# Flamingo gated block on one Trainium2 core: LayerNorm statistics of x blocks 1 to 3 taken in steps 0 and 1 of segment 0, and context block 1 copied out between the first two exponentials

## What is computed

```python
x = x + tanh(g_xattn[0]) * xattn(layernorm(x), ctx_1024, ...)
x = x + tanh(g_ffn[0]) * ffn(layernorm(x), w_gate, w_up, w_down)
# xattn: 16 heads of 64
lat = layernorm(latents, ln_l_w, ln_l_b)     # latents: layernorm(x)
ctx = layernorm(context, ln_c_w, ln_c_b)
q = lat @ Wq;  k, v = split(ctx @ Wkv)
attn = softmax(clip(q @ k.T * 64**-0.5, -11, 11))
out = (attn @ v) @ Wo + bo
# ffn: fake-quantised gate, up and down products, 768 wide
```

## Time and profile before

| | |
|---|---|
| Time, median of 3 runs | 1176.95 us (1175.2 to 1177.44) |
| Profiled execution, its own time | 1177.15 us |
| Its span | 1175.3 us, 20655 instructions |
| PE busy | 1098.6 us, 93% |
| DVE busy | 976.0 us, 83% |
| ACT busy | 622.0 us, 53% |
| POOL busy | 34.1 us, 3% |
| DMA | 22.24 MB, mean 19 GB/s |
| PE clock granted, mean | 0.979 of full |

### The profile page before, as it was taken

One profiled execution on the slowest core, in us unless ns is written; L12 is line 12 of the kernel. 1 busy time (PEld: TensorE's weight loads), 2 busy tenths in 40 slices (PEclk: granted clock), 3 DMA queues, 4 the chain that ended last, 5 costly groups with the idle time before them and its releaser, 6 DMA issues.

```text
span 1175.3 us, 20655 instructions
## 1 busy us (share of the span) xinstructions
PE 1098.6 (93%) x8548; PEld 507.3 (43%) x8548; DVE 976.0 (83%) x1336; ACT 622.0 (53%) x719; POOL 34.1 (3%) x41
## 2 busy tenths in 40 slices
PE   5899999999999999999999999999999998999049
PEld 3443344434443444344434443444333332787049
DVE  7667978797879788988989888987888899849996
ACT  3455555555555555555555555555555555449652
POOL 0400000000000000000000000000000000003200
PEclk9999999999999999999999999999999999999579
DMA  5000300010001000100010001000000000000002
GB/s 168 1 1 2 117 1 19 1 37 2 20 1 37 1 19 2 37 1 20 1 37 1 20 1 38 1 20 1 20 10 11 10 11 10 1 1 1 0 1 73
DMA packets 27324, 22.24 MB, mean 19 GB/s; under 512 B 8477, under 2 KB 23006, under 8 KB 27230
## 3 DMA queue, kind: packets, MB, share of 16 engines
q1 hardware_dynamic: 27230, 20.92, 5.8%
HBM read 18.55 MB, written 2.22 MB: 18 GB/s over the span
## 4 chain that ended last, share of the span: by engine, by line
PE 81%; DVE 7%; ACT 4%; issue 4%; POOL 0%; POOLq 0%; DVEq 0%; ACTq 0%
PE ps L1145 29%; PE ps L1129 28%; PE ps L1028 5%; PE ps L1081 4%; PE ps L1038 3%; PE ps L1047 3%; PE ps L1247 3%; PE ps L1292 3%; DVE acc L785 2%; PE ps L1058 1%; DVE gt L955 1%; ACT z L609 1%; ACT z L611 1%; DVE e_buf L829 1%; DVE fst L672 1%
## 5 line engine op out<-in xcount | busy, mean ns | idle before, releaser
L531 ACT ACTIVATE e_buf<-ps 128x1024 f32<-128x1024 f32 x416 | 426.5, 1025 | 319.4 <-PE ps L1129 319.4
L1145 PE MATMUL ps<-e_buf,vb 64*64 64x512 f32 x3328 | 436.1, 594 | 4.4 <-DVE e_buf L829 4.2
L785 DVE TENSOR_TENSOR acc<-acc,e_buf 128x1024 f32<-128x1024 f32 (+1 forms) x352 | 428.1, 1216 | 0.0
L829 DVE TENSOR_SCALAR e_buf<-e_buf 128x1024 f32<-128x1024 f32 x416 | 284.0, 683 | 96.5 <-ACT e_buf L531 96.4
L1145 PEld LDWEIGHTS ps<-e_buf,vb 64*64 64x64 f32 x3328 | 120.3, 133 | 243.6 <-issue 212.6
L1129 PE MATMUL ps<-qb,kb_odd 64*64 64x512 f32 x1664 | 216.0, 589 | 0.0
L1129 PE MATMUL ps<-qb,kb_even 64*64 64x512 f32 x1664 | 215.9, 589 | 0.0
L1129 PEld LDWEIGHTS ps<-qb,kb_odd 64*64 64x64 f32 x1664 | 63.8, 133 | 114.7 <-issue 114.4
L1129 PEld LDWEIGHTS ps<-qb,kb_even 64*64 64x64 f32 x1664 | 63.7, 133 | 114.3 <-issue 114.2
L821 DVE TENSOR_TENSOR xacc<-ps,xacc 128x512 f32<-128x512 f32 x60 | 41.4, 692 | 56.3 <-PE ps L1081 56.3
L1247 PE MATMUL ps<-hT,wgu 128*128 128x512 f32 x288 | 67.7, 396 | 0.1
(11 more groups left out here) (126 smaller groups left out, 636.1 us busy)
## 6 DMA issues: line engine op xcount, KB each, us to landing
rden<-inv_rows SPq DMA_DIRECT2D x62, 128.0 KB, 2.8
xacc<-in_x_dram SPq DMA_DIRECT2D x4, 512.0 KB, 7.0
wst<-in_L_xattn_Wkv_dram SPq DMA_DIRECT2D x16, 128.0 KB, 2.7
out_dram<-z SPq DMA_DIRECT2D x7, 256.0 KB, 2.2
wst<-in_L_xattn_Wq_dram SPq DMA_DIRECT2D x8, 128.0 KB, 2.7
wo_raw<-in_L_xattn_Wo_dram SPq DMA_DIRECT2D x8, 128.0 KB, 3.5
acc<-in_ctx_dram SPq DMA_DIRECT2D x2, 512.0 KB, 7.1
den_spread<-den_row SPq DMA_DIRECT2D x62, 2.0 KB, 1.7
```

Source lines behind the costliest of these rows:

```text
L531: nc.scalar.activation(e_buf[:, g % E_BUFS, :, :], sc[:, g % 2, :, :], ACT.Exp, scale=float(DH) ** -0.5).then_inc(exp_done, 1)
L785: dve.tensor_tensor(acc[0:r, t0 % 3, :, :], a, e_buf[0:r, (ST * t0 + st) % E_BUFS, :, :], ALU.add).then_inc(summed, 1)
L829: dve.tensor_scalar(tile, tile, EXP_LO, EXP_HI, ALU.max, ALU.min).then_inc(clip_done, 1)
L1145: ins = pe.matmul(ps_o[DH * h:DH * h + DH, half, :], vb[rows, p % 2, st, DH * h:DH * h + DH], e_buf[rows, g % E_BUFS, h, :], start=(st == ...
```

## The change

Two things move; no instruction's size or count changes, except that some are grouped otherwise.

```diff
                     if t0 == 0:
-                        if st == 1:
+                        if st == 0:
                             ctx_take(1)
...
                 if st == 0:
                     normalise(ctx_at(12), crows[12:], crows[12:], ctx_norm)
-                if 1 <= st < NBS:
-                    moments(lat_at(4 * st), lrows[4 * st:4 * st + 4], {0: in_x[st]})
-                if st == NBS - 1:
+                    moments(lat_at(4), lrows[4:8], {0: in_x[1]})
+                if st == 1:
+                    moments(lat_at(8), lrows[8:], {0: in_x[2], 4: in_x[3]})
                     inverse_root((lat_at(4), LN3, *twice))
```

## The result

The changed kernel takes 1172.35 us (median of 6 runs, 1171.86 to 1174.62) against 1177.31 for the kernel before beside it (median of 6, 1175.2 to 1178.43). The ratio is 0.9963, with a 95% interval of 0.995 to 0.9976: 4.4 us faster, between 2.8 and 5.9. The interval comes from comparing all twelve runs and is wide, since the runs of the changed kernel fall into two groups, 1171.9 to 1172.4 and 1174.0 to 1174.6. In the profiled execution the span is 1170.4 us, 4.9 less.

A forecast was written before the change was run, and what follows sets the result against it. PE was taken to bound the kernel (81% of the chain). Copy 0.44, POOL's wait 2.86 and clock 1.52 sum to 4.82 us, giving 1172.1 us from the median 1176.95; range 1170.6 to 1174.4.

The forecast's parts named there:

- What bounds it: Whole kernel: PE is 81% of the chain; reachable are its waits of 0.71 and 3.17 us and the lowered clock.
- Copy a step earlier, 0.44: Context block 1's copy on ACT follows the first exponential, needing four of eight transposes: 0.44 us gained, bounds 0 to 0.71.
- POOL's start 7.3 us earlier: Normalisations of x begin at 34.4 instead of 41.71 us; four tiles done by 41, at worst 41.9; POOL's wait goes whole.
- The wait left behind a copy, 0.31 of 3.17: Ahead of the z transposes, PE still waits 0.31 us for ACT's copy of k: gain 2.86, bounds 2.70 to 3.17.
- The clock, 1.52: From the first z transpose to scores(7), granted clock stays 1.00 instead of 0.50: gain 1.52 us, bounds 0 to 1.6.
- The rival that short waits bring the fall: PE's long wait goes but several short waits still lower the clock: only 3.30 us gained, 1173.6; chance 0.06.
- DVE's late clips, at nothing: Clip of step 2 ends at 34.8 us, behind the root chain; values(2) wants it at 40.0, slack 5.2, cost nothing.
- The Trainium skill's rule on the shared port: DVE and GpSimd lock one port pair per instruction; POOL's tiles could hold DVE's backlog 3.3 us, to 43.0 instead of 39.7.
- That the shift reaches the end: From 48 us on PE is the chain in every later segment, so the whole 4.82 us arrives at the end.

The follow-up runs named there:

- e2: Kernel before with only the copy of context block 1 moved, to between the first exponentials; 1176.7 us, ratio 0.9993, step 0's scores to segment 1's k job 0.42 us shorter.
- e4: Changed kernel with the statistics kept in steps 0 and 1 but the root chain in step 3 as before; 1172.58 us, ratio 0.9963 to the kernel before.
- e9: Kernel before with 12 extra identity matmuls on PE while it waits for POOL ahead of the z transposes; 1175.77 us, ratio 0.9988.
- e3: Kernel before with 26 extra identity matmuls on PE during its wait for POOL, taking 6.07 us, twice the wait; 1179.17 us, ratio 1.0017.

## Why the prediction was right

The forecast was 1172.1 us, 4.82 less; the median is 1172.35, and 4.80 less in the stretch. That the median lies within 0.3 us of the forecast is in part luck, since the runs spread over 2.8 us and the interval of the gain is 2.8 to 5.9; the agreement of the stretch and of its terms is what counts.

- **What bounds it.** PE's two waits and its clock account for the whole: by the rows 0.41 up to the k job, 2.85 from there to the transposes, 1.55 from there to the scores, and nothing (23.65 us against 23.66) from there to the end of the stretch.
- **Copy a step earlier, 0.44.** Measured 0.42 (0.71 - 0.29, and e2's stretch). ACT waited 0.39 us for PE, and the first copy began 0.70 us behind the first of the eight transposes (forecast 0.67), which take 1.09 together. So it did not wait for all eight, as the prediction chose.
- **POOL's start 7.3 us earlier.** It was 7.76 by the trace's clock, 0.35 of which is PE's and ACT's earlier arrival in this execution. DVE's part of it, 7.4, is 0.1 over the forecast. Four tiles were done at 40.5 (forecast 41, at worst 41.9), and the cover was 4.2 us. e4 shows that it could be shorter.
- **The wait left behind a copy, 0.31 of 3.17.** Measured 0.31, with the releaser named. Gain 2.86, as predicted.
- **The clock, 1.52.** From the first transpose to the scores it is 46.61 - 44.71 = 1.90 us against 3.45, so 1.55; e9 gives 1.53 by itself. One reading was a little off: PE had been idle for 3.0 us and not for 3.17 when the clock fell, since the windows of before put the fall at 48.1 (the mean from 48 to 49 us is 0.57). It changes nothing in the sum. The rival that short waits bring the fall did not come true with those in segment 0, up to 0.71 us, but e4 has such a fall elsewhere (below).
- **DVE's late clips, at nothing.** The clip of step 2 ended at about 34.3 and PE took values(2) at 39.70, again without a wait.
- **The Trainium skill's rule on the shared port.** The Trainium skill's page "SBUF — State Buffer", section "SBUF: two separate sides", lets a POOL instruction that starts first hold DVE too. Here a clip took 1.00 us at 42.78, beside a POOL tile, instead of 0.69, and POOL's tiles took 2.43 and 3.08 us beside DVE's backlog: both sides of it show, much more on POOL's. The backlog itself was not held: it ended at 39.18, by the rows forecast for 39.7, and not at the 43.0 that the prediction worked out by the page's rule. The longer clips cost nothing, since PE never waited for one between 20 and 80 us.
- **That the shift reaches the end.** Behind the last long wait of PE before the final product the lead was 1129.45 - 1124.24 = 5.21 us, of which 0.35 comes from the start. 0.3 of it was lost after that (below). The prediction had no term for either; in the profiled pair they all but cancel.

## What to carry to other kernels

Read the wait of the bounding engine, then walk its releaser's queue back to what could have run earlier: here twelve POOL instructions waited for three blocks' statistics that sat behind clips nobody needed yet. A wait of the matmul engine costs more than its length if the granted clock falls behind it; matmuls of nothing, sized to fit the wait (e9, not e3), return that part alone, and tell how large it is. Where whole runs spread as much as the effect, measure between two fixed instructions that enclose the change.

## What the hardware showed unexpectedly

- **The start varies by 1.1 us.** The scores of step 0 began anywhere from 21.98 to 23.13 us, in kernels whose program is the same up to there. The first k job of four matmuls took 1.98 to 3.03 us. The profile gives the granted clock as 1.00 in that time, though the first eight transposes took 1.94 us where eight at 24 us took 1.09; so the record does not show the clock's start, and that this is the clock is argued, not shown.
- **The clock's return at the end varies too.** PE idles for 26 us before the final product. Behind that come two groups of matmuls on the identity, which compute nothing. The 20 records of the second took 2.40 us in the kernel before, at a granted clock of 1.00, and 3.95 in the changed one, where it was 0.59 on average. Most of these 1.55 us were covered, since PE then waited 0.64 and 0.85 us for its operands before and 0.20 after: the last long group (L1292, 252 records) begins at 1142.93 and 1138.02, so the lead is 4.91 us there, 0.3 less. First the rows of before, then those of after:

```profile
1129.45 4.21 PE L1223 MATMUL ps<-ident 128*128 128x128 f32 x18 [26.20 <-DVE gt L955]
1134.57 2.40 PE L1223 MATMUL ps<-ident 128*128 128x128 f32 x20
```

```profile
1124.24 4.21 PE L1223 MATMUL ps<-ident 128*128 128x128 f32 x18 [26.19 <-DVE gt L955]
1129.62 3.95 PE L1223 MATMUL ps<-ident 128*128 128x128 f32 x20
```

- **The clock can fall behind waits of about 1 us.** The profiled execution of e4 took 1174.3 us and one other run 1174.26, the remaining three 1172.1 to 1172.6. Its clock is 0.52 in 994 to 996 us, behind waits of 0.72 and 1.25 us for DVE; the changed kernel has the same waits there and kept its clock. Values of eight matmuls took 1.98 us in place of 1.09, and from their start to the 64-row products (L1101, L1102 in e4) it is 6.25 us against 4.62: the fall cost 1.6 us. The windows of e4:

```profile
992.00:994.00 2.00, 0.81 (x8) 0.00 (x0) 2.00 (x4) 1.03 (x3) 0.00 (x0) 1.00 0.00 0
994.00:996.00 2.00, 1.94 (x9) 0.33 (x9) 1.97 (x3) 0.00 (x0) 0.00 (x0) 0.52 0.00 0
```

Since the changed kernel's own runs lie at 1171.9 to 1172.7 and at 1174.0 to 1174.6, this may be most of the 2 us that part them; only e4's trace shows it, so it stays open.
